# The seam between attention and MLP on one core: mask, bound and means moved, last chunks reordered

## The reference

```python
q = _l2norm(proj(Wq)); k = _l2norm(proj(Wk)); v = proj(Wv)
attn = softmax(q k^T + bias)            # query i sees keys i .. i+127
x = _layernorm(x + (attn v) Wo^T)
...
bw = mean(abs(w), axis=1) * sign(w)     # for w1 and for w2
h = gelu(x bw1^T + b1)
x = _layernorm(x + h bw2^T + b2)
```

## Time and profile before

| | |
|---|---|
| median of 3 runs | 403.35 us (402.19 to 403.46) |
| the profiled execution | 402.48 us |
| its span on the core | 400.7 us, so 1.78 us lie around it |
| granted TensorE clock | 0.984 of full speed, 1.00 in every stretch of the seam |
| PE, DVE, ACT, POOL busy | 92%, 78%, 78%, 70% |

### The profile page before, as it was taken

The page is one execution under the profiler, slowest core; times in us unless marked ns, Lnnn a source line. Parts: engine busy times, 40 slices in busy tenths (PEclk is TensorE's granted clock), DMA queues, the critical chain, the costliest instruction groups (busy, mean ns, idle before and its releaser), DMA issues. The chain is left out here.

```text
span 400.7 us, 11989 instructions
## 1 busy us (share of the span) xinstructions
PE 370.3 (92%) x3893; PEld 232.4 (58%) x3893; DVE 311.8 (78%) x854; ACT 312.5 (78%) x532; POOL 280.1 (70%) x424
## 2 busy tenths in 40 slices
PE   7588999999999999999999899889899999999991
PEld 5234655665566556655665556555566666666671
DVE  4964777687777877877778978646789988998985
ACT  3678787878887888788878778679888888888754
POOL 2387888888888888888888879969156635645321
PEclk9789999999999999999999999999999999999996
DMA  6687457643554355436533555431032126303112
GB/s 229 131 238 125 107 106 141 142 89 79 111 117 87 79 118 117 79 81 122 111 79 80 104 101 121 81 61 40 2 55 53 55 53 106 92 12 105 53 54 105
DMA packets 98542, 38.28 MB, mean 96 GB/s; under 512 B 84688, under 2 KB 97360, under 8 KB 98256
## 3 DMA queue, kind: packets, MB, share of 16 engines
q1 hardware_dynamic: 98512, 37.89, 42.9%
HBM read 12.72 MB, written 4.19 MB: 42 GB/s over the span
## 5 line engine op out<-in xcount | busy, mean ns | idle before, releaser
L1149 POOL TENSOR_SCALAR_AFFINE_SELECT prob<-prob 128x512 f32<-128x512 f32 x256 | 157.1, 645 | 34.8 <-ACT prob L601 34.8
L601 ACT ACTIVATE prob<-ps 128x1024 f32<-128x1024 f32 x128 | 127.3, 1027 | 3.1 <-PE ps L338 3.1
L365 PE MATMUL ps<-wqkv,xt 128*128 128x512 f32 x128 | 67.5, 615 | 2.3 <-DVE qkn L863 1.9
L511 PE MATMUL ps<-sgn,prob 128*128 128x256 f16 x512 | 61.5, 273 | 1.1 <-DVE prob L970 0.9
L485 PE MATMUL ps<-yT,sgn 128*128 128x512 f16 x256 | 61.1, 379 | 0.6 <-issue 0.6
L665 ACT ACTIVATE ps<-ps,bias,alpha 128x512 f32<-128x512 f32 x64 | 47.8, 750 | 15.6 <-PE ps L485 12.4
L511 PEld LDWEIGHTS ps<-sgn,prob 128*128 128x128 f16 x512 | 50.0, 98 | 14.4 <-DVE prob L970 2.6
L1206 POOL TENSOR_TENSOR resid<-z,resid 128x256 f32 (+1 forms) x31 | 22.6, 728 | 49.5 <-DVE z L980 49.5
L354 PE MATMUL ps<-prob,vdiag 128*17 128x128 f32 x1024 | 51.3, 274 | 2.5 <-POOL prob L1149 2.4
L338 PEld LDWEIGHTS ps<-qkT 64*128 64x128 f16 x512 | 17.7, 95 | 61.2 <-issue 34.6
L338 PE MATMUL ps<-qkT 64*128 64x256 f16 x512 | 45.8, 276 | 6.3 <-DMA qkT<-parts 5.2
(11 more groups left out here) (106 smaller groups left out, 578.2 us busy)
## 6 DMA issues: line engine op xcount, KB each, us to landing
xt<-in_xT SPq DMA_DIRECT2D x32, 128.0 KB, 2.9
resid<-in_x SPq DMA_DIRECT2D x32, 128.0 KB, 2.2
out_dram<-resid SPq DMA_DIRECT2D x7, 512.0 KB, 2.9
w_t<-in_w2T SPq DMA_DIRECT2D x1, 1024.0 KB, 8.4
w_t<-in_w1T SPq DMA_DIRECT2D x1, 1024.0 KB, 5.3
w_nat<-in_w SPq DMA_DIRECT2D x4, 256.0 KB, 4.8
wqkv<-in_wqkvT SPq DMA_DIRECT2D x3, 256.0 KB, 3.8
qkT<-parts SPq DMA_TRANSPOSE x32, 4.3
```

Of the source, the lines that this page charges most:

```text
L365: mm = nc.tensor.matmul(ps[:, QK[1 - par], :], xt[:, slot, k, :], wqkv[:, k, 0:2 * D], start=(k == 0), stop=(k == DC - 1))
L511: mm = nc.tensor.matmul(ps[:, banks[b], 0:D], hid[:, par, a, k, P * b:P * b + P], sgn2[:, k, :], start=(m == 0), stop=(m == 2 * HC - 1))
L601: nc.scalar.activation(prob[:, par, CH * c:CH * c + CH, :], ps[:, SC + 2 * (c % 2):SC + 2 * (c % 2) + 2, :], ACT.Exp, scale=QK_SCALE ** -2 ...
L1149: sel = nc.gpsimd.affine_select(out=at, in_=at, compare_op=ALU.is_ge, fill=0.0, base=-near, pattern=[[0, CH], [1 if near else -1, P]], cha ...
```

## The change

Nothing is computed differently; operations change places.

- The bound's first part moves from ahead of step 26 to ahead of step 27; its transpose, `take_bound` and the spread move from step 26 to step 28; the second part from ahead of step 27 to ahead of step 29. The three PSUM places change with them.
- The means' matmul moves behind step 31, into v's bank, and L947 onto VectorE's list behind step 31. `hidden(0, 0)` now waits for the bound alone.
- GpSimd masks all four chunks of step 29 before `low_halves`. In step 31 it cuts the half that the step's own sums read first, and the half of `weighted_sum(NB, ...)` later, with a semaphore of its own, `own_cut`.
- In the tail, `weighted_sum(NB, ...)` stands ahead of `project_out(NB)`; ScalarE's and VectorE's lists are reordered.
- The first group runs three hidden chunks ahead of the first second-layer sum (3, 2, 2, 1 in place of 2, 2, 2, 2), and the waits that stood ahead of the whole group stand inside `second`.

```diff
-        mean_at, turned_at, bound_at = ps[:, 0, 0:D], ps[0:1, 0, D:D + P], ps[:, 0, D + P:D + P + 1]
+        turned_at, bound_at, mean_at = ps[0:1, 0, 0:P], ps[:, 0, P:P + 1], ps[:, VO, 0:D]
...
             def turn_bound():
-                pe.wait_ge(prep, 1)
                 pe.wait_ge(bound_done, 1)
-                pe.wait_ge(qkn_done, NB - 3)
-                nc.tensor.matmul(mean_at, mean_ones[:], w2_sum[:], start=True, stop=True)
+                pe.wait_ge(qkn_done, NB - 1)
                 nc.tensor.transpose(turned_at, bound1[:], id32[:]).then_inc(bound_turned, 1)
...
-                pe.wait_ge(prep, 2)
+                pe.wait_ge(abs_done, 7)
                 hidden(0, 0, 0)
...
+            def means():
+                pe.wait_ge(prep, 1)
+                pe.wait_ge(v_ready, NB)
+                pe.wait_ge(resid_done, NB - 2)
+                nc.tensor.matmul(mean_at, mean_ones[:], w2_sum[:], start=True, stop=True).then_inc(means_done, 1)
...
+                if isinstance(g, int) and g == 0:
+                    if b == 0:
+                        pe.wait_ge(hlo_done, 1)
+                    elif b == 1:
+                        pe.wait_ge(resid_done, NB)
...
-            step(NB - 6, 0, 2, between=turn_bound, before_pv=spread_bound)
-            step(NB - 5, 1, 3, between=means_taken)
-            step(NB - 4, 0, 0)
+            step(NB - 6, 0, 2)
+            step(NB - 5, 1, 3)
+            step(NB - 4, 0, 0, between=turn_bound, before_pv=spread_bound)
...
+            means()
             hidden(0, 3, 0)
...
-            project_out(NB, False)
             for c in range(NC):
                 weighted_sum(NB, c, 0, False)
+            pe.wait_ge(prep, 2)
+            project_out(NB, False)
...
-            pe.wait_ge(hlo_done, 1)
-            pe.wait_ge(resid_done, NB)
-            group_step(0, 0)
+            for b, chunks in enumerate(((0, 1, 2), (3, 4), (5, 6), (7,))):
+                for k in chunks:
+                    hidden(1, k, 1)
+                second(0, b, 0)
...
             act.wait_ge(abs_done, 6)
+            take_strips(NB)
             gelu_of(0, 0, 0)
             gelu_of(0, 1, 0)
-            take_strips(NB)
-            act.wait_ge(prep, 2)
+            act.wait_ge(abs_done, 9)
+            take_rows(NB)
             high_hidden(0, 1, 0)
             gelu_of(0, 2, 0)
             gelu_of(0, 3, 0)
-            take_rows(NB)
+            take_strips(NB + 1)
             high_hidden(0, 3, 0)
             gelu_of(0, 4, 0)
-            take_strips(NB + 1)
+            take_rows(NB + 1)
             gelu_of(0, 5, 0)
             high_hidden(0, 5, 0)
-            take_rows(NB + 1)
...
-            step(NB - 3, 1, early2=True)
+            step(NB - 3, 1)
...
-            step(NB - 1, 1, next2=False)
+            for c, near in ((0, 1), (1, 1), (0, 0), (2, 1), (3, 1), (1, 0), (2, 0), (3, 0)):
+                cut_tile(NB - 1, c, 1, near).then_inc(cut_ready if near else own_cut, 1)
```

More of the change, by code:

```diff
@@ L214, in build @@
         prep = sem("prep")
-        sgn_ready, bias_ready = sem("sgn_ready"), sem("bias_ready")
+        sgn_ready, bias_ready, means_done = sem("sgn_ready"), sem("bias_ready"), sem("means_done")
+        own_cut = sem("own_cut")
         abs_done = sem("abs_done")
@@ L348, in weighted_sum @@
                     count(pe, ot_ready, i - 1)
-                pe.wait_ge(cut_ready, i * NC + c + 1 if cur else NB * NC)
+                if cur:
+                    pe.wait_ge(cut_ready, i * NC + c + 1)
+                else:
+                    pe.wait_ge(own_cut, c + 1)
                 tiles = [1 - par, par] if cur else [1 - par]
@@ L491, in first_hidden @@
                 pe.wait_ge(sgn_ready, 2)
-                pe.wait_ge(prep, 2)
+                pe.wait_ge(abs_done, 7)
                 hidden(0, 0, 0)
-            def means_taken():
-                pe.wait_ge(prep, 2)
+            def means():
[3 more added lines that the diff above has]
+                nc.tensor.matmul(mean_at, mean_ones[:], w2_sum[:], start=True, stop=True).then_inc(means_done, 1)
             def second(g, b, par, banks=ZBANKS):
@@ L923, in _ @@
             step(NB - 7, 1, aside=lambda: abs_w1(1))
+            step(NB - 6, 0)
             dve.wait_ge(abs_done, 2)
@@ L934, in _ @@
             nc.vector.tensor_reduce(bound1[:], bound[:], AX.X, ALU.max).then_inc(bound_done, 1)
-            step(NB - 6, 0, aside=take_bound)
+            step(NB - 5, 1)
+            step(NB - 4, 0, aside=take_bound)
             dve.wait_ge(bound_all, 1)
@@ L945, in _ @@
                                     ALU.mult, ALU.add).then_inc(abs_done, 1)
[L946 to L949, removed]
             step(NB - 3, 1, next3=False)
@@ L1105, in _ @@
             row_stats(NB - 4, mv_late[:, 0, :])
+            dve.wait_ge(means_done, 1)
+            dve.wait_ge(abs_done, 10)
+            nc.vector.tensor_scalar(alpha2[:], mean_at, h_unscale[:], Y_SCALE, ALU.mult, ALU.mult).then_inc(prep, 1)
+            outputs(NB)
             hidden_low(0, 0, 0)
-            outputs(NB)
             hidden_low(0, 1, 0)
@@ L1110, in _ @@
             add_output(NB)
+            outputs(NB + 1)
             hidden_low(0, 3, 0)
-            outputs(NB + 1)
             hidden_low(0, 4, 0)
+            add_output(NB + 1)
             hidden_low(0, 5, 0)
-            add_output(NB + 1)
             hidden_low(0, 6, 0)
@@ L1139, in _, with cut_tile @@
             nc.gpsimd.memset(qkT[:, QSLOT[XS - 1], 0:H // 2], 0.0).then_inc(consts, 1)
-            def cut_chunk(i, c, par):
+            def cut_tile(i, c, par, near):
+                tile = 1 - par if near else par
                 chunks = pool.to_reg(i * NC + c + 1)
@@ L1146, in cut_chunk @@
                 pool.wait_ge(exp_done, chunks)
[L1147 to L1152, removed]
+                at = prob[:, par, CH * c:CH * c + CH, P * tile:P * tile + P]
+                return nc.gpsimd.affine_select(out=at, in_=at, compare_op=ALU.is_ge, fill=0.0, base=-near,
+                                               pattern=[[0, CH], [1 if near else -1, P]],
+                                               channel_multiplier=-1 if near else 1)
+            def cut_chunk(i, c, par):
+                cut_tile(i, c, par, 0)
+                cut_tile(i, c, par, 1).then_inc(cut_ready, 1)
             def low_halves(i, par):
```

## The result

The changed kernel takes 400.63 us (median of 5 runs, 399.75 to 401.38), the kernel before 403.35 on the same chip: a ratio of 0.994, 95% interval 0.992 to 0.996. A later comparison on another chip gave 0.9951 (0.9932 to 0.997) for the same kernel. The forecast was 401.7 with 400.2 to 403.1. The profiled execution has 400.63 us and a span of 398.9, clock 0.986.

A forecast was written before the change was run, and what follows sets the result against it. Waits passing from engine to engine, none above 19%, were taken to bound the kernel. Step 31 ending 2.2 us earlier, less 0.6 lost in the tail, gave −1.6: median 403.35 to 401.7 us, range 400.2 to 403.1.

The forecast's parts named there:

- Step 26: Without the bound's first part ahead, `turn_rows` comes 0.85 us earlier and L462's 0.3 falls away; step 27 starts 1.16 earlier.
- Step 27: The bound's first part, 1.3 us, now stands here: stall 0.7 against 0.5 that falls away, net +0.2 us.
- rival 1: Step 27: VectorE waits for GpSimd's instructions again, stall 1.2 in place of 0.7: 402.2 us; chance 0.27 shared with other rivals.
- The upper bound, 1.66: Step 27: longest time in us for the bound's first part, if its wait for GpSimd is met again in full.
- Steps 28, 29, 31: Step 28 +0.4 us for L457 and L462; step 29 −1.4 by earlier GpSimd cuts; step 31 −0.26 by an earlier cut.
- rival 3: Step 29's stall returns as a wait for block 31's transpose: 0.4 us at 6.0 to landing (402.1); shared chance 0.27.
- Rival 4: Block 31's transpose landing beyond 8.4 us undoes the whole gain; at 10 us the kernel ends at 404.6; chance 0.06.
- The tail: TensorE leaves the next group's first sum 0.5 to 0.6 us later, as ScalarE's 1.33 us lateness makes VectorE 0.6 late.
- the forecast's middle: Whole kernel: 400.9 to 402.1 us, chance 0.55.
- rival 2's better half: End of the tail's seam: the low halves do not bind and TensorE keeps its 0.6 us: 400.5 us; chance 0.12.

The follow-up runs named there:

- the reordered tail: The change with ScalarE's first GELU ahead of the strips, VectorE's first high half ahead of the means, groups 2, 2, 2, 2: 400.07 us (0.9919), again 399.24 (0.992).

## Why the prediction was right

**Step 26:** predicted −1.16, measured 9.89 to 8.73, −1.16, with the border at 233.79. `turn_rows` came at 228.44 (228.57 predicted; the 0.13 is the earlier start of the step): VectorE's `double` waits for GpSimd's `low_halves`, as read from step 25. The prediction left out one wait, and it cost nothing: the transpose for step 27's scores, issued at 227.86, landed 6.1 us later, and TensorE starts them 0.21 late, at 234.00. The trace of before shows the same transpose issued at 228.00 and landing after 6.1, so at 234.1, when step 27 was forecast for 233.92. The 0.18 us for which `turn_strips` otherwise waits for ScalarE fell away in exchange. From start to start the step gave −0.96, and step 27 −0.03.

**Step 27:** predicted +0.2 with a stall of 0.7, measured +0.18 with 0.63 (by the same border). The part cost 1.28 (1.3 chosen between 0.95 and 1.66, so the size is partly luck). Two operations met GpSimd's instructions, each for less than L931 had. So rival 1 held as a mechanism, not at its price. The Trainium skill (page "SBUF — State Buffer", section "Who interferes with whom") has VectorE with two SBUF inputs wait while GpSimd reads SBUF. The trace agrees: both end within 0.03 us of GpSimd's instruction. The upper bound, 1.66, did not come, since each was caught for the rest of such an instruction only. (The prediction gives L931's neighbours 0.15 us; L927 took 0.34, and ends at 226.02 where a GpSimd instruction does at 225.99.)

**Steps 28, 29, 31:** predicted +0.4, −1.4 and −0.26; measured +0.37, −1.38 and −0.28. The end of step 31 came 2.23 us earlier (66.15 to 63.92), predicted 2.2. The wait of step 31's scores for the transpose (rivals 3 and 4) did not come: it was issued at 260.44 and landed 4.3 us later, 1.2 ahead of the scores at 265.96. Rival 4's prices do not follow from rival 3's rule. By that rule, one us of time for each us beyond 5.6 to landing, the gain is gone near 7.3 us, not 8.4, and 10 us give 406.1, not 404.6.

**The tail:** predicted +0.5 to 0.6, measured 0.55 and 0.43 in two profiles; TensorE leaves the second group's first sum 28.34 us behind step 31's end (301.26), before 27.91 (303.19). The total is close, and its steps are partly mis-sized. TensorE entered the first group 0.90 earlier, not 0.6: the tail had 1.28 us of idle time, and all of it went. ScalarE was 1.17 late at 285.39, not 1.33, and the copy started 17.48 us behind step 31's end, not 17.95. So VectorE's low half started at 18.23, 0.2 later than before, not 0.6. The other 0.27 came further on: L769 took 0.62 in place of 0.37 for its line of before, and ends at 293.10 as a GpSimd instruction does at 293.07. By 299.68 VectorE was 0.47 late, and this reached TensorE. The forecast counted that lateness in the wrong place. The two waits it named at the last matmuls of that sum are there (0.61 and 0.38 us).

**What it did not see:** that the tail's loss was one order on one engine. ScalarE waits 0.90 ahead of its first copy and 1.24 ahead of `take_rows`, with two ready GELUs behind. Putting its four copies behind GELUs that are ready brings it to its first GELU of the group 11.0 us behind step 31's end in place of 13.1, and takes 1.4 to 1.5 us off the kernel. Which of the four moves counts most was not run. Nor was TensorE's exchange, the own half's sum ahead of the projection, by itself.

The sum was −1.6 us against a profiled 402.48; the profiled executions differ by 1.85 and the medians by 2.7. The two pieces of the profile give −1.68, so the prediction's working covers the profile. The remaining 1.0 of the medians is not explained by it. The same kernel measured 2.0 us below before in the second comparison, so a spread between comparisons is likely. For the same reason 400.63 lies below the 400.9 to 402.1 of the forecast's middle, in the part given to rival 2's better half. That rival's mechanism did not hold: the low halves do bind (0.61 and 0.38 us). The median is better than the working for a reason that is not in it.

## What to carry to other kernels

In hand-written lists, look for an engine that stands idle ahead of an instruction while ready work is queued behind it: here GELUs moved ahead of ScalarE's four copies gave 1.4 us, more than the moved bound and means (0.62). Before an engine's list is changed, ask what its new first instruction waits for: ScalarE's new order alone gave the tail's whole gain by the profile, while VectorE's alone, which begins with a wait for ScalarE's first GELU, cost 2.5. And side work that fits into no gap comes back as a stall in the same step or the next: here 1.1 to 1.3 us of it left stalls of 0.60 to 0.71 us in steps 26, 27 and 29.

## What the runs showed of the hardware

The start of the program does not always go the same way. TensorE at the scores of an early step, and the stretches from 34 to 38 us, in the first profile of the reordered tail:

```profile
35.93 1.04 PE L339 MATMUL ps<-qkT 64*128 64x256 f16 x8 [2.71 <-DMA qkT<-parts]
```

```profile
34.00:36.00 2.00, 0.07 (x2) 0.10 (x4) 0.29 (x1) 0.00 (x0) 0.29 (x1) 0.86 0.27 58
36.00:38.00 2.00, 2.00 (x13) 1.52 (x14) 0.00 (x0) 1.42 (x2) 0.26 (x1) 0.50 1.15 215
```

and of its second profile, the same kernel:

```profile
33.69 0.61 PE L339 MATMUL ps<-qkT 64*128 64x256 f16 x8 [0.99 <-DMA qkT<-parts]
```

```profile
34.00:36.00 2.00, 2.00 (x16) 0.83 (x12) 1.13 (x5) 1.88 (x2) 0.72 (x2) 1.00 0.33 65
36.00:38.00 2.00, 2.00 (x12) 1.00 (x11) 0.31 (x1) 1.58 (x4) 1.76 (x4) 1.00 1.25 210
```

A transpose that lands about 2 us later (the longest there takes 7.1 us from issue to landing, in the second profile 5.4) leaves TensorE idle for 2.71 us, against 0.99; behind that the granted clock is 0.50, the lower level of 1.2 GHz, where the other profile has 1.00. In the runs of the kernel before in that comparison, four had a mean clock of 0.980 to 0.981 and took 403.86 to 404.35 us; the eleven at 0.984 to 0.985 took 401.94 to 403.36. That these four began in the same way is likely, but was not profiled. It is as large as most of the effects studied here, which is why the table compares pieces of the profile.
